# One decoder layer on one core: the calls of all five engines' programs in another sequence, with other fillers on TensorE

## The chip, the cores and the metric

The kernel runs on one NeuronCore of one Trainium2 chip. The metric is the device time of the whole program in microseconds (us); it counts from the first to the last activity on the core, with some 1.3 us around the span that the profile shows.

## The reference

The input x is 16 batches of 256 tokens by 512 channels, ctx a second tensor of the same shape. Cut to what matters:

```python
x = x + attention(layernorm(x))        # 16 heads of 32, one shared key and value head
x = x + wkv(w, u, layernorm(x), ctx)   # recurrence over the 256 tokens of a batch
x = x + ffn(layernorm(x))              # ternary weights, 2048 hidden units

# attention: windows of 128 queries, step 64, blended linearly where they overlap
K, V = quant_dequant_8bit(K), quant_dequant_8bit(V)   # min and max over ALL batches
p = sigmoid(scores); wout = (p / (p.sum(-1) + 1e-8)) @ V
# wkv: y = (A*p + E*vt) / (A*q + E), per channel, state carried from token to token
# ffn: activations rounded to 8 bit with a scale per token, weights to -1, 0, 1 with
#      one scale per matrix (a mean of absolute values), silu(gate) * up, RMS norm, down
```

Two facts of this set the order of the work at the start: keys and values are quantised with a minimum and maximum over all batches, so all of x must be loaded and projected before the first scores; and a weight can be rounded only when the sum over its whole matrix is known.

## The kernel before

The 16 batches are pipelined. Round b does the attention of batch b, the wkv of batch w = b−1, the first half (tokens 0 to 127, t = 0) of the hidden part of the FFN of f = b−2, and the second half (t = 1) of the hidden part and the down projection of g = b−3. Rounds 0 to 3 fill the pipeline and are written out call by call, rounds 4 to 15 are the body of a loop (`for i in range(4, B)`), and a tail empties it.

Each engine has a program of its own, a list of calls of small step functions written out by hand: `sync_program` (SP, which issues most DMAs), `tensor_program` (PE), `scalar_program` (ACT), `vector_program` (DVE) and `pool_program` (POOL). An engine does its steps strictly in the order of its list; steps of different engines meet only at semaphores. So a step that waits holds all that stands behind it in its own list. DMAs on SP's queue are issued in the order of SP's list, and each waits for its own condition first.

The steps that matter here, with the lines by which the profile names them:

- PE: `queries(b, t)` L558 projects the queries (with the residual's path folded in); `scores(b, h)` L577 for a group of four heads; `dens` L585 and `nums` L588 sum the probabilities and multiply them with the values; `attention_out` L608; `wkv_keys` L618 and `wkv_back` L627 transpose to and from the layout of the recurrence; `gate_up(f, t, n)` L646 is a chunk of 512 hidden units, eight products of gate and eight of up; `down(f, t, k)` L666 is half of the sum over the hidden units.
- PE's fillers: `spin(f, k, n)` L658 issues n products of a constant matrix into a bank that is free at that time. Nobody reads them. Each shows as two records in the trace.
- ACT: `keep_raw` L893 to 906 writes projected keys and values of two batches, `sum_weights` L914 adds up a chunk of 128x2048 weights, `set_keys` L928 dequantises keys; `probs` L945 is the sigmoid; `log_tables` L949 loads the function table for `logs` L956 and `inverses` L961 (a logarithm and an exponential that together make the reciprocal); `wkv_logs`, `wkv_inverses` L966, L971 do the same for the recurrence; `scale_tokens` L978, `scale_hidden` L984, `exps` L991, `silu` L1000, `squares` L1005.
- DVE: `round_weights` L1292 to 1301 makes ternary weights, three passes a chunk; `rope` L1378, `rotate` L1384, `blend_windows` L1392, `residual` L1402, `scan` L1425, `join` L1433, `refine` L1439, `quotient` L1446, the `wkv_...` steps up to L1492, `hidden(f, t, n)` L1503 (silu times up, out of PSUM), `peak` L1512, `hidden_scale` L1525, `hidden_round` L1532, `output` L1537.
- POOL: `weigh_windows` L1846, `weigh_hidden` L1863, `hidden_rstd` L1869, `outputs` L1883.
- SP: `load_x` L270 and `load_columns` L276 (x and its transpose, 1.05 MB a call), `load_weights` L293 (1.05 MB), `load_queries` L305, `load_residual` L300 (0.52 MB), `load_keys` L317, `turn_queries` L330, `turn_tokens` L337, `turn_hidden` L344 (transposes by DMA), `store` L351.

The fillers' code:

```python
def spin(f, k, n):
    if k >= 4:
        te.wait_ge(silu_set.sem, silu_set.at(f, (k - 4) // 2))
    ...
    for _ in range(n):
        te.matmul(bank[4 + k % 4][:, 0:S], ident[:, :], blend[:, 0:S], start=True, stop=True)
```

## Time and profile before

| | |
|---|---|
| time, median of 3 runs | 1019.5 us (1018.1 to 1020.02) |
| the profiled execution | 1018.47 us, its span 1017.2 us |
| PE, DVE busy | 899.2 us (88%), 876.8 us (86%) |
| ACT, POOL busy | 657.0 us (65%), 427.2 us (42%) |
| fillers (L658) | 318 records, 75.3 us of PE |

The profile is of one execution. The page divides the span into 40 slices and gives busy shares, bandwidth and the clock that TensorE was granted; the trace behind it has each instruction, and for idle time in front of an instruction the one whose semaphore ended it. Busy shares are averages over three stages: the start, the steady rounds, the tail.

### The profile page before, as it was taken

How to read it: one execution, taken by the hardware profiler on the slowest of the kernel's cores; microseconds unless marked ns; L12 is line 12 of the kernel's file. 1: busy time of each engine (PE TensorE's matmuls, PEld its weight loads, DVE VectorE, ACT ScalarE, POOL GpSimd, SP SyncE). 2: the span in 40 equal slices, each digit the busy share in tenths (PEclk: the TensorE clock that was granted, in tenths of full speed). 3: DMA queues.
4: the chain of work that ended last, by engine and by line, in shares of the span. 5: the costliest groups of instructions: out<-in, count | busy, mean ns of one | idle time of the engine just before them, and what ended most of it. 6: DMA issues, size and time to landing. Idle time of an engine off the chain costs nothing.

```text
span 1017.2 us, 22672 instructions
## 1 busy us (share of the span) xinstructions
PE 899.2 (88%) x8616; PEld 559.4 (55%) x8706; DVE 876.8 (86%) x1614; ACT 657.0 (65%) x1163; POOL 427.2 (42%) x494
## 2 busy tenths in 40 slices
PE   4997969977789998989898989898989898988898
PEld 2446657754455555555555555565555555555354
DVE  2866694799899999999999999989898989889884
ACT  0238554366666868686868685859585959595653
POOL 1200213116344454545454545454535363636452
PEclk9999989978899999999999999999999999999999
DMA  9986560020331323232323232415151515131132
GB/s 330 362 348 194 199 208 26 17 65 16 73 102 43 111 63 111 56 112 61 107 66 105 68 108 63 112 57 119 53 123 53 122 53 123 53 85 53 42 73 83
DMA packets 119389, 107.21 MB, mean 105 GB/s; under 512 B 91792, under 2 KB 94720, under 8 KB 118128
## 3 DMA queue, kind: packets, MB, share of 16 engines
q1 hardware_dynamic: 116320, 100.64, 33.1%
q0 software_dynamic: 624, 2.59, 0.7%
q10 hardware_dynamic: 2336, 2.52, 0.7%
q8 instruction: 69, 1.13, 0.5%
q14 instruction: 40, 0.33, 0.1%
HBM read 65.62 MB, written 10.75 MB: 75 GB/s over the span
## 4 chain that ended last, share of the span: by engine, by line
PE 37%; ACT 17%; POOL 14%; DVE 12%; issue 12%; DMA 2%; SPq 1%; DVEq 0%; POOLq 0%; ACTq 0%
PE bank L558 10%; PE bank L666 6%; POOL work L1863 5%; PE bank L646 5%; POOL sums L1846 4%; ACT arena L945 4%; PE bank L577 4%; PE bank L658 3%; PE bank L608 3%; ACT junk L1000 2%; ACT L949 2%; PE bank L585 2%; DVE wide L1358 2%; DVE amax L1468 2%; POOL sums L1883 2%
## 5 line engine op out<-in xcount | busy, mean ns | idle before, releaser
L1863 POOL TENSOR_TENSOR work<-junk,lnw 128x512 f32<-128x512 f32 x128 | 171.1, 1356 | 201.6 <-DVE junk L1503 176.8
L646 PE MATMUL bank<-w_up_gate,qT 128*128 128x512 bf16 x974 | 231.7, 383 | 19.1 <-DVE junk L1503 10.9
L646 PEld LDWEIGHTS bank<-w_up_gate,qT 128*128 128x128 bf16 x1024 | 95.6, 98 | 128.3 <-DVE junk L1503 21.7
L984 ACT ACTIVATE work<-work,fs 128x2048 f32<-128x2048 f32 x32 | 64.0, 2001 | 118.3 <-DVE fs L1525 118.3
L945 ACT ACTIVATE arena<-bank 128x384 f32<-128x384 f32 x256 | 104.8, 497 | 33.5 <-PE bank L577 33.3
L666 PE MATMUL bank<-w_down,work 128*128 128x512 bf16 x472 | 114.4, 387 | 11.3 <-ACT junk L1000 5.1
L558 PE MATMUL bank<-wide,wq_sb 128*128 128x256 f32 x512 | 114.5, 381 | 2.5 <-DVE rows L1402 2.5
L608 PE MATMUL bank<-wo_sb,wide 128*128 128x512 f32 x256 | 112.7, 592 | 1.2 <-DVE wide L1395 1.2
L558 PEld LDWEIGHTS bank<-wide,wq_sb 128*128 128x128 f32 x512 | 96.1, 190 | 26.0 <-issue 13.4
L577 PE MATMUL bank<-wide,k_win 32*128 32x128 f32 x1536 | 64.1, 298 | 47.1 <-ACT arena L945 23.4
L1005 ACT ACTIVATE junk<-junk 128x512 f32<-128x512 f32 x128 | 80.3, 627 | 39.2 <-DVE junk L1503 38.9
L1846 POOL TENSOR_TENSOR sums<-sums,blend 128x448 f32<-128x448 f32 x64 | 84.2, 1333 | 42.7 <-ACT sums L961 42.6
L1000 ACT ACTIVATE junk<-bank,deq 128x512 f32<-128x512 f32 x128 | 84.5, 681 | 23.7 <-PE bank L646 11.5
L1503 DVE TENSOR_TENSOR junk<-bank,junk 128x512 f32<-128x512 f32 x128 | 86.3, 683 | 13.1 <-POOL work L1863 8.1
L577 PEld LDWEIGHTS bank<-wide,k_win 32*128 32x128 f32 x1536 | 51.9, 195 | 74.7 <-ACT arena L945 42.9
L666 PEld LDWEIGHTS bank<-w_down,work 128*128 128x128 bf16 x512 | 46.5, 99 | 62.1 <-issue 6.3
L608 PEld LDWEIGHTS bank<-wo_sb,wide 128*128 128x128 f32 x256 | 48.5, 190 | 56.5 <-issue 53.1
L1425 DVE TENSOR_TENSOR_SCAN sums<-wkv_s,sums 128x256 f32<-128x256 f32 x128 | 77.8, 674 | 0.2 <-ACT sums L991 0.2
L658 PE MATMUL bank<-blend,ident 128*128 128x256 f32 x318 | 75.3, 390 | 0.0
L1512 DVE TENSOR_REDUCE fs<-work 128x1 f32<-128x2048 f32 x32 | 72.9, 2277 | 1.7 <-POOL work L1863 1.7
L1883 POOL TENSOR_TENSOR sums<-sums 128x512 f32<-128x512 f32 x32 | 41.0, 1283 | 73.5 <-ACT sums L971 66.0
L658 PEld LDWEIGHTS bank<-blend,ident 128*128 128x128 f32 x318 | 61.2, 195 | 11.4 <-issue 1.9
(156 smaller groups left out, 1614.0 us busy)
## 6 DMA issues: line engine op xcount, KB each, us to landing
sums<-in_xT SPq DMA_DIRECT2D x8, 1024.0 KB, 9.4
wide<-in_xT SPq DMA_DIRECT2D x16, 512.0 KB, 4.7
wide<-wide SPq DMA_DIRECT2D x64, 128.0 KB, 2.1
out<-rows SPq DMA_DIRECT2D x32, 256.0 KB, 2.3
rows<-in_x SPq DMA_DIRECT2D x15, 512.0 KB, 3.5
ctx_T<-in_ctxT SPq DMA_DIRECT2D x15, 512.0 KB, 3.7
...
```

The costliest lines, as they stand in the source:

```text
L558: last = te.matmul(in_bank(k, 2)[:, n % 2, :], wq_sb[:, c, n * P:(n + 1) * P], xT[:, c, :], start=c == 0, stop=c == NC - 1)
L577: last = te.matmul(bank[j][:, n * P:(n + 1) * P], k_win[head, window], q_cos[head, c, window], start=True, stop=True, skip_group_check=True)
L608: last = te.matmul(bank[t][:, :], heads_T[:, c, t * P:(t + 1) * P], wo_sb[:, c, :], start=c == 0, stop=c == NC - 1)
L646: last = te.matmul(bank[4 + k % 4][:, :], qT[:, c, t * P:(t + 1) * P], w_up_gate[:, m, c, cols], start=c == 0, stop=c == NC - 1)
L658: te.matmul(bank[4 + k % 4][:, 0:S], ident[:, :], blend[:, 0:S], start=True, stop=True)
L666: last = te.matmul(bank[6 + t][:, :], hid_T[:, t, c, :], w_down[:, c, :], start=c == 0, stop=c == NI - 1)
L945: se.activation(prob[:, :, QUAD * c + j, :], bank[j][:, 0:NW * P].rearrange("p (k q) -> p k q", k=NW), ACT.Sigmoid, scale=float(1.0 / np.s ...
L1000: se.activation(gated[:, n % 2, :], bank[4 + 2 * (n % 2)][:, :], ACT.Silu, scale=deq[:, 0, t:t + 1]).then_inc(silu_set.sem, 1)
L1005: se.activation(gated[:, n % 2, :], hid[:, n % 2, :], ACT.Square, accum_out=fs[:, t, n:n + 1]).then_inc(sq_set.sem, 1)
L1503: ve.tensor_tensor(hid[:, n % 2, :], bank[4 + k % 4][:, :], gated[:, n % 2, :], op=ALU.mult).then_inc(hid_set.sem, 1)
L1846: ge.tensor_tensor(soft[:, c, :], soft[:, c, :], blend[:, :], op=ALU.mult).then_inc(weighted.sem, 1)
L1863: ge.tensor_tensor(hid_w[:, t, cols], hid[:, n % 2, :], lnw[:, cols], op=ALU.mult).then_inc(z_set.sem, 1)
```

## The change

Every engine's list is written in another sequence. The steps are the same ones, with two exceptions: the number and places of the filler products change, and so does which of ACT's function tables is loaded when (the explicit load `log_tables(2, 0)` goes from round 2 to the head of the list). Calls at the loop's seams move from one side of its edge to the other. The core of the diff (left out are the rest of the start of DVE's and POOL's lists, and those of their tails):

```diff
@@ -377,110 +377,109 @@
             for t in range(NT):
                 sy.wait_ge(out_stored[t].sem, out_stored[t].at(B - 1))
 
-        load_x(1)
         load_columns(0)
-        load_columns(2)
         load_small()
         load_x(0)
+        load_x(1)
+        load_columns(2)
         load_columns(1)
         load_x(2)
         load_x(3)
         load_columns(3)
         load_x(4)
-        load_columns(5)
         load_columns(4)
         store_trig(0)
         load_x(5)
+        load_x(6)
+        load_columns(5)
+        load_x(7)
         load_columns(6)
-        load_x(6)
+        store_trig(2)
+        load_columns(7)
         load_wq()
-        load_keys(0)
-        load_columns(7)
-        load_x(7)
-        load_weights(GATE, 2)
+        load_queries(0)
+        next_residual(1)
         load_weights(GATE, 0)
         load_weights(GATE, 1)
-        load_queries(0)
+        load_weights(GATE, 3)
         store_trig(3)
-        load_weights(GATE, 3)
+        load_weights(GATE, 2)
+        load_keys(0)
         turn_queries(0, 0)
...
         queries(0, 0)
         queries(0, 1)
-        spin(0, 0, 5)
+        spin(0, 0, 6)
         scores(0, 0)
-        spin(0, 0, 6)
+        spin(0, 0, 7)
         scores(0, 1)
+        spin(0, 0, 1)
         scores(0, 2)
         spin(0, 0, 2)
         scores(0, 3)
+        spin(0, 0, 8)
         dens(0, 0)
         dens(0, 1)
+        nums(0, 0)
         dens(0, 2)
-        nums(0, 0)
+        spin(0, 0, 3)
         dens(0, 3)
-        spin(0, 0, 7)
+        spin(0, 0, 4)
         nums(0, 1)
         nums(0, 2)
-        spin(0, 0, 10)
+        spin(0, 0, 5)
         nums(0, 3)
         attention_out(0, 0)
         attention_out(0, 1)
-        spin(0, 0, 8)
         queries(1, 0)
         queries(1, 1)
+        spin(0, 0, 9)
         wkv_keys(0)
+        spin(0, 0, 15)
         scores(1, 0)
-        spin(0, 0, 4)
+        spin(0, 0, 10)
         scores(1, 1)
+        spin(0, 0, 11)
         scores(1, 2)
-        spin(0, 0, 3)
+        spin(0, 0, 12)
         scores(1, 3)
         dens(1, 0)
+        spin(0, 0, 13)
         dens(1, 1)
+        spin(0, 0, 14)
         dens(1, 2)
-        spin(0, 0, 9)
+        dens(1, 3)
         nums(1, 0)
-        spin(0, 0, 11)
         nums(1, 1)
-        dens(1, 3)
         nums(1, 2)
-        spin(0, 0, 12)
         nums(1, 3)
+        spin(0, 0, 16)
         wkv_back(0, 0)
         wkv_back(0, 1)
         attention_out(1, 0)
-        spin(0, 0, 13)
+        spin(0, 0, 17)
         attention_out(1, 1)
         queries(2, 0)
-        spin(0, 2, 7)
+        spin(0, 0, 18)
+        gate_up(0, 0, 0)
+        queries(2, 1)
         wkv_keys(1)
...
         for i in range(4, B):
-            b, w, f, g, h = i, i - 1, i - 2, i - 3, i - 4
+            b, w, f, g = i, i - 1, i - 2, i - 3
+            dens(w, 0)
+            dens(w, 1)
+            gate_up(g, 1, 0)
             dens(w, 2)
-            down(h, 1, 1)
             nums(w, 0)
             nums(w, 1)
             dens(w, 3)
             nums(w, 2)
+            nums(w, 3)
             gate_up(g, 1, 1)
-            nums(w, 3)
             gate_up(g, 1, 2)
             wkv_back(f, 0)
             wkv_back(f, 1)
@@ -811,6 +815,7 @@
             gate_up(f, 0, 1)
             wkv_keys(w)
             gate_up(f, 0, 2)
+            spin(f, 6, 2)
             gate_up(f, 0, 3)
             scores(b, 0)
             down(g, 0, 0)
@@ -819,17 +824,17 @@
             scores(b, 2)
             down(g, 1, 0)
             scores(b, 3)
-            gate_up(f, 1, 0)
-            dens(b, 0)
-            dens(b, 1)
+            down(g, 1, 1)
...
@@ -849,11 +853,12 @@
         down(13, 0, 1)
         down(13, 1, 1)
         gate_up(14, 1, 1)
+        spin(14, 12, 5)
         gate_up(14, 1, 2)
         wkv_back(15, 0)
         wkv_back(15, 1)
         gate_up(14, 1, 3)
-        spin(14, 16, 19)
+        spin(14, 16, 18)
         gate_up(15, 0, 0)
         gate_up(15, 0, 1)
         gate_up(15, 0, 2)
@@ -866,10 +871,9 @@
         gate_up(15, 1, 1)
         gate_up(15, 1, 2)
         gate_up(15, 1, 3)
-        spin(15, 16, 2)
         down(15, 0, 0)
         down(15, 0, 1)
-        spin(15, 16, 14)
+        spin(15, 16, 19)
         down(15, 1, 0)
...
+        log_tables(2, 0)
         load_tables()
         keep_raw(0)
         keep_raw(1)
         keep_raw(2)
         keep_raw(3)
         keep_raw(4)
-        wkv_tables()
         load_first_residual()
-        load_first_values()
+        sum_weights(GATE, 0)
         keep_raw(5)
-        sum_weights(GATE, 0)
         keep_raw(6)
         keep_raw(7)
         sum_weights(GATE, 1)
         sum_weights(GATE, 2)
+        sum_weights(GATE, 3)
+        wkv_tables()
         set_keys(0)
-        sum_weights(GATE, 3)
         probs(0, 0)
         probs(0, 1)
-        log_tables(0, 0)
         probs(0, 2)
         probs(0, 3)
+        log_tables(0, 0)
         logs(0, 0)
+        sum_weights(UP, 0)
         inverses(0, 0)
         logs(0, 1)
-        sum_weights(UP, 0)
         logs(0, 2)
+        load_first_values()
         logs(0, 3)
...
         silu(0, 0, 2)
-        squares(0, 0, 1)
         silu(0, 0, 3)
         probs(2, 0)
+        log_tables(1, 0)
         probs(2, 1)
+        squares(0, 0, 2)
         probs(2, 2)
-        squares(0, 0, 2)
...
         for i in range(4, B):
             b, w, f, g = i, i - 1, i - 2, i - 3
-            silu(g, 1, 1)
-            silu(g, 1, 2)
-            squares(g, 1, 1)
-            silu(g, 1, 3)
+            scale_tokens(f)
             scale_hidden(g, 0)
-            squares(g, 1, 2)
             set_keys(b)
-            scale_tokens(f)
-            squares(g, 1, 3)
             scale_hidden(g, 1)
             silu(f, 0, 0)
             silu(f, 0, 1)
@@ -1172,13 +1176,13 @@
             logs(b, 3)
             inverses(b, 3)
             silu(f, 1, 0)
+            silu(f, 1, 1)
             squares(f, 1, 0)
-        silu(13, 1, 1)
-        silu(13, 1, 2)
-        squares(13, 1, 1)
-        silu(13, 1, 3)
-        squares(13, 1, 2)
-        squares(13, 1, 3)
+            silu(f, 1, 2)
+            squares(f, 1, 1)
+            silu(f, 1, 3)
+            squares(f, 1, 2)
+            squares(f, 1, 3)
...
@@ -1614,11 +1618,11 @@
         wkv_quantise(0)
         residual(1)
         wkv_round(0)
+        round_weights(DOWN, 0)
         att_norm(1)
         wkv_steps(0)
-        round_weights(DOWN, 0)
+        hidden(0, 0, 0)
         round_weights(DOWN, 1)
-        hidden(0, 0, 0)
         rope(2, 0)
...
         for i in range(4, B):
             b, w, f, g, h = i, i - 1, i - 2, i - 3, i - 4
+            join(f)
             keys_grid(b)
             peak(g, 0)
             refine(f, 0)
+            output(h, 0)
             refine(f, 1)
             output(h, 1)
             quotient(f, 0)
@@ -1703,58 +1707,58 @@
             hidden_round(g, 0)
             hidden(f, 0, 0)
             rope(b, 0)
+            hidden(f, 0, 1)
             hidden_round(g, 1)
-            hidden(f, 0, 1)
             rope(b, 1)
             rotate(b, 0)
+            scan(w, 0)
             values(w)
-            scan(w, 0)
+            rotate(b, 1)
             scan(w, 1)
-            rotate(b, 1)
             hidden(f, 0, 2)
             hidden(f, 0, 3)
-            output(g, 0)
-            join(w)
+        join(14)
+        peak(13, 0)
```

The first place is in TensorE's list, at attention_out of batch 0 (L608, L607 after the change) and the scores, sums and products of batch 1 behind it. Before:

```order
L608 MATMUL bank<-wo_sb,wide 128x512 x8
L658 MATMUL bank<-blend,ident 128x256 x8
L558 MATMUL bank<-wide,wq_sb 128x256 x16
L618 MATMUL bank<-ident,wide 128x128 x8
L577 MATMUL bank<-wide,k_win 128x128 x12
L658 MATMUL bank<-blend,ident 128x256 x4
L577 MATMUL bank<-wide,k_win 128x128 x24
L658 MATMUL bank<-blend,ident 128x256 x3
L577 MATMUL bank<-wide,k_win 128x128 x12
L585 MATMUL bank<-arena,one_win 32x128 x12
```

After:

```order
L607 MATMUL bank<-wo_sb,wide 128x512 x8
L557 MATMUL bank<-wide,wq_sb 128x256 x16
L657 MATMUL bank<-blend,ident 128x256 x9
L617 MATMUL bank<-ident,wide 128x128 x8
L657 MATMUL bank<-blend,ident 128x256 x15
L576 MATMUL bank<-wide,k_win 128x128 x12
L657 MATMUL bank<-blend,ident 128x256 x10
L576 MATMUL bank<-wide,k_win 128x128 x12
L657 MATMUL bank<-blend,ident 128x256 x11
L576 MATMUL bank<-wide,k_win 128x128 x12
L657 MATMUL bank<-blend,ident 128x256 x12
L576 MATMUL bank<-wide,k_win 128x128 x12
```

Ahead of and among the scores and the sums stand 9, 15, 10, 11, 12, 13 and more filler products where 8, 4, 3, 9 and more stood.

The second place is in TensorE's list too, in a steady round: gate_up(f, 0, 2) and (f, 0, 3), the scores of batch b with down between them, and the sums of batch b behind them. Before:

```order
L646 MATMUL bank<-w_up_gate,qT 128x512 x16
L577 MATMUL bank<-wide,k_win 128x128 x12
L666 MATMUL bank<-w_down,work 128x512 x8
L577 MATMUL bank<-wide,k_win 128x128 x12
L666 MATMUL bank<-w_down,work 128x512 x8
L577 MATMUL bank<-wide,k_win 128x128 x12
L666 MATMUL bank<-w_down,work 128x512 x8
L577 MATMUL bank<-wide,k_win 128x128 x12
L646 MATMUL bank<-w_up_gate,qT 128x512 x8
L585 MATMUL bank<-arena,one_win 32x128 x12
L588 MATMUL bank<-arena,one_win 32x64 x4
```

After:

```order
L645 MATMUL bank<-w_up_gate,qT 128x512 x8
L657 MATMUL bank<-blend,ident 128x256 x2
L645 MATMUL bank<-w_up_gate,qT 128x512 x8
L576 MATMUL bank<-wide,k_win 128x128 x12
L665 MATMUL bank<-w_down,work 128x512 x8
L576 MATMUL bank<-wide,k_win 128x128 x12
L665 MATMUL bank<-w_down,work 128x512 x8
L576 MATMUL bank<-wide,k_win 128x128 x12
L665 MATMUL bank<-w_down,work 128x512 x8
L576 MATMUL bank<-wide,k_win 128x128 x12
L665 MATMUL bank<-w_down,work 128x512 x8
L584 MATMUL bank<-arena,one_win 32x128 x12
```

Two fillers stand between gate_up(f, 0, 2) and (f, 0, 3), the last half of down comes before the first sums, and gate_up(f, 1, 0) between the second and third instead of ahead of the first.

The third place is the end of TensorE's list: the last chunks of gate_up of batch 15 and its down. Before:

```order
L646 MATMUL bank<-w_up_gate,qT 128x512 x40
L666 MATMUL bank<-w_down,work 128x512 x32
L646 MATMUL bank<-w_up_gate,qT 128x512 x24
L658 MATMUL bank<-blend,ident 128x256 x2
L666 MATMUL bank<-w_down,work 128x512 x16
L658 MATMUL bank<-blend,ident 128x256 x14
L666 MATMUL bank<-w_down,work 128x512 x16
```

After:

```order
L645 MATMUL bank<-w_up_gate,qT 128x512 x40
L665 MATMUL bank<-w_down,work 128x512 x32
L645 MATMUL bank<-w_up_gate,qT 128x512 x24
L665 MATMUL bank<-w_down,work 128x512 x16
L657 MATMUL bank<-blend,ident 128x256 x19
L665 MATMUL bank<-w_down,work 128x512 x16
```

The two fillers ahead of down are gone, and 19 stand between its halves instead of 14.

## Rows read from the trace of the kernel before

**Rows 1.** The page: its head, and the bandwidth of the 40 slices.

```profile
span 1017.2 us, 22672 instructions
...
GB/s 330 362 348 194 199 208 26 17 65 16 73 102 43 111 63 111 56 112 61 107 66 105 68 108 63 112 57 119 53 123 53 122 53 123 53 85 53 42 73 83
```

**Rows 2.** TensorE timeline: start us, us, line, out<-in, count [idle before <-releaser].

```profile
14.68 1.56 PE L534 MATMUL bank<-arena 128*128 128x96 f32 x6 [14.68 <-DMA arena<-in_low_rank]
...
74.25 7.13 PE L558 MATMUL bank<-wide,wq_sb 128*128 128x256 f32 x32
...
115.78 7.13 PE L608 MATMUL bank<-wo_sb,wide 128*128 128x512 f32 x16 [1.20 <-DVE wide L1395]
...
141.13 1.24 PE L577 MATMUL bank<-wide,k_win 32*128 32x128 f32 x16 [6.98 <-DVE wide L1384]
...
185.40 3.60 PE L608 MATMUL bank<-wo_sb,wide 128*128 128x512 f32 x8
```

**Rows 3.** ScalarE timeline at 67 us, columns as in the group before.

```profile
67.40 1.91 ACT L914 ACTIVATE junk<-work 128x2048 f32<-128x2048 f32 x1 [0.41 <-ACT q_tok L904]
```

**Rows 4.** ScalarE groups, 84.9 to 115.8 us: count | busy, mean ns | idle before.

```profile
L945 ACT ACT_TABLE_LOAD x2 | 2.6, 1283 | 1.8 <-PE bank L577 1.8
L956 ACT ACT_TABLE_LOAD x2 | 2.6, 1283 | 0.0
L961 ACT ACT_TABLE_LOAD x2 | 2.6, 1283 | 0.0
L956 ACT ACTIVATE sums<-bank,sum_eps 128x448 f32<-128x448 f32 x4 | 2.4, 630 | 0.0
L949 ACT ACT_TABLE_LOAD x1 | 1.3, 1283 | 0.0
```

**Rows 5.** Windows: stretch, PE, PEld, DVE, ACT, POOL busy, PEclk, DMA share, GB/s.

```profile
115.80:189.00 73.20, 61.87 (x553) 47.12 (x554) 51.62 (x84) 32.01 (x53) 15.12 (x16) 0.95 0.28 92
189.00:313.80 124.80, 104.15 (x1015) 66.69 (x1026) 112.28 (x182) 77.02 (x135) 49.93 (x53) 0.90 0.19 56
```

**Rows 6.** Windows of line L658 alone: PE, PEld busy, PEclk, DMA share, GB/s.

```profile
115.78:189.03 73.25, 28.44 (x120) 23.03 (x120) 0.95 0.28 92
```

**Rows 7.** VectorE timeline, 199 to 204 us.

```profile
199.77 1.28 DVE L1292 TENSOR_SCALAR work<-work,w_scale 128x2048 f32<-128x2048 f32 x1
...
202.35 1.23 DVE L1301 TENSOR_SCALAR w_down<-work 128x2048 bf16<-128x2048 f32 x1
203.49 0.68 DVE L1503 TENSOR_TENSOR junk<-bank,junk 128x512 f32<-128x512 f32 x1
```

**Rows 8.** TensorE timeline: two waits of rounds 2 and 3.

```profile
238.65 1.25 PE L585 MATMUL bank<-arena,v_win 128*32 128x128 f32 x17 [4.14 <-ACT sums L956]
...
260.16 1.03 PE L646 MATMUL bank<-w_up_gate,qT 128*128 128x512 bf16 x4 [1.26 <-DMA qT<-q_tok]
```

**Rows 9.** TensorE timeline, a steady round at 534 us.

```profile
533.94 1.04 PE L646 MATMUL bank<-w_up_gate,qT 128*128 128x512 bf16 x4 [0.67 <-DVE junk L1503]
...
535.93 0.95 PE L577 MATMUL bank<-wide,k_win 32*128 32x128 f32 x24 [0.95 <-DVE wide L1384]
```

**Rows 10.** The chain that ended last: start us, us, engine, line.

```profile
313.84 7.13 PE bank L558 x32
...
519.22 7.14 PE bank L558 x32
...
570.55 7.14 PE bank L558 x32
...
589.28 4.11 DMA wide<-wide
...
879.78 7.14 PE bank L558 x32
```

**Rows 11.** TensorE timeline, the tail.

```profile
1004.18 6.21 PE L658 MATMUL bank<-blend,ident 128*128 128x256 f32 x28
1010.68 1.46 PE L666 MATMUL bank<-w_down,work 128*128 128x512 bf16 x6 [0.30 <-DMA work<-work]
```

More of the change, by code:

```diff
@@ L1084, in scalar_program @@
         wkv_logs(1, 0)
+        logs(2, 1)
         wkv_logs(1, 1)
         wkv_inverses(1, 0)
+        inverses(2, 1)
         wkv_inverses(1, 1)
[L1088 removed]
         logs(2, 2)
         silu(0, 1, 0)
[L1091 to L1093 removed]
+        inverses(2, 2)
         logs(2, 3)
[L1095 removed]
         inverses(2, 3)
         silu(0, 1, 1)
+        squares(0, 1, 0)
         silu(0, 1, 2)
         squares(0, 1, 1)
+        silu(0, 1, 3)
         squares(0, 1, 2)
[L1101 to L1102 removed]
         scale_hidden(0, 0)
         scale_tokens(1)
+        squares(0, 1, 3)
         set_keys(3)
@@ L1574, in vector_program @@
         rotate(0, 0)
-        rotate(0, 1)
         weight_mean(GATE)
         round_weights(GATE, 0)
+        rotate(0, 1)
         round_weights(GATE, 1)
         round_weights(GATE, 2)
+        round_weights(GATE, 3)
         blend_windows(0, 0)
-        round_weights(GATE, 3)
+        keys_grid(1)
         blend_windows(0, 1)
@@ L1591, in vector_program @@
         rope(1, 0)
+        rope(1, 1)
         round_weights(UP, 2)
-        rope(1, 1)
         rotate(1, 0)
+        round_weights(UP, 3)
         values(0)
-        round_weights(UP, 3)
+        rotate(1, 1)
         scan(0, 0)
-        rotate(1, 1)
         scan(0, 1)
```

294 lines of the change are left out of this document (142 added, 152 removed).

## The prediction

> **What bounds the kernel now.** I read the page first, then the chain that ended last, then timelines of each engine stretch by stretch. The page's head gives a span of 1017.2 us; the profiled execution took 1018.5 in all, and the median of the runs shown is 1.0 above that, so my sum is made on 1018.5 and gets 1.0 added at its end. The bandwidth row shows the first stage: three slices at 330 to 362 GB/s [rows 1], with nearly all of x under way. No score can start before x is in. The chain then shows the steady rounds by their anchor, the 32 products of queries: 313.84 to 879.78 us are 11 rounds, 51.45 us each, an undisturbed one (519.22 to 570.55) 51.33 [rows 10]. Between lies the filling of the pipeline, 81.4 us (end of queries(0, ·), 74.25 + 7.13) to 313.8 [rows 2, 10], and the change touches this most.
>
> In that filling two stretches differ. From 115.8 to 189.0 TensorE is busy 61.87 of 73.20 us, of which 28.44 us are fillers that nobody reads; from 189.0 to 313.8 VectorE is the full one, 112.28 of 124.80 us [rows 5, 6]. In a steady round no engine is always busy: a loop of hand-overs goes from queries over gate_up, silu and the sigmoids to the reciprocals of the recurrence, POOL's products, VectorE's rounding and back to queries.
>
> **The change, stage by stage.**
>
> *1. Start to the end of queries(0, ·): −2.7.* The first products wait for low_rank [rows 2], which goes out behind x1, col0 and col2 (3.1 MB) and in future behind col0 alone. Two loads of 1.05 MB and what POOL loads beside them, together 2.5 MB, at 347 GB/s (mean of the first three slices, [rows 1]) make 7.2 us by which projections can start earlier. But all of x must come, and its bytes are the same. GATE weight 0 lands behind x, its transpose, wq, 0.5 MB for queries and 0.5 for the residual, about 21.4 MB with the small loads: at 347 GB/s and 2 us to begin, 63.7 us. Its sum now stands ahead of keep_raw(5) on ScalarE, where today it starts at 67.40, right behind keep_raw(5)'s copies [rows 3]; so keep_raw(5) can't be done much before 66 us. load_keys(0) stands behind all four weights. Bounds: −7.2 (nothing of it lost) and 0; I take −2.7, nearer to nothing, since keep_raw(5) by this sum comes when it comes now.
>
> *2. To the start of attention_out(0, 0): −3.7.* ScalarE loads its table seven times between 84.9 and 115.8 us, each 1.28 us [rows 4], as log_tables(0, 0) stands between the second and third sigmoid group and the later sigmoids throw its table out. Behind all four groups it is loaded twice: 5 fewer, −6.4. ScalarE is what the sums wait for here. Fillers in the stretch go from 30 to 36. A filler costs 28 records / 2 = 14 in 6.21 us, 0.444 us [rows 11]; six are +2.7. Bounds −6.4 and +2.7.
>
> ScalarE's next activation follows a load with no idle time [rows 4]. The Trainium skill (ScalarE: Activation LUTs, What ACT_TABLE_LOAD costs) puts a drain of some 1.38 us to each load, 2.66 in all; by that the five would give −13.3 and the sum would be 6.9 us lower. No such gap shows in the rows, and the sum goes by them.
>
> *3. attention_out(0, 0) to the end of attention_out(1, 1): +12.8.* This is the main term. Now it is 115.78 to 185.40 + 3.60 = 189.0, 73.2 us [rows 2]. Fillers in it: 8+4+3+9+11+12+13 = 60 (120 records, 28.44 us); in future 9+15+10+11+12+13+14+16+17 = 117. TensorE's list is strict, and these products depend on nothing that comes late, so they are a floor: 117 × 0.444 = 51.9. The other work of the stretch is 61.87 − 28.44 = 33.4 [rows 5, 6]. Together 85.3, and 0.7 for short waits: 86.0. The 11.3 us that TensorE idles now, 6.98 of them ahead of the scores at 141.13 [rows 2], are thereby filled up and overrun. Bounds: 85.3 − 73.2 = +12.1, if no wait is left, and +57 × 0.444 = +25.3, if all waits stay. They can't: 24 fillers (10.7 us) now stand ahead of scores(1, 0), where rope and rotate cost a wait of 6.98.
>
> *4. To hidden(0, 0, 0): +3.7.* From 189.0 to hidden's start at 203.49 are 14.5 us [rows 2, 7]. In future 18 fillers (8.0) instead of 7 (3.1) stand ahead of gate_up(0, 0, 0), while wkv_keys (1.1) goes behind it: gate_up starts some 3.8 us later, and as hidden is held today by round_weights up to 203.58 and not by TensorE [rows 7], it comes at the same distance. But VectorE's list has hidden(0, 0, 0) ahead of round_weights(DOWN, 1): it waits for TensorE first, and the chunk, three passes from 199.77 to 203.58, 3.8 us [rows 7], is still to do, with VectorE the full engine of what follows. Bounds 0 (the late TensorE gives VectorE slack elsewhere) and +3.8; I take +3.7.
>
> *5. To queries(4, ·) at 313.84: −4.0.* TensorE's wait of 4.14 us for logs(2, 3) [rows 8] goes, since squares(0, 1, 0) and a table load no longer stand ahead of it on ScalarE; the 1.26 us for a transpose of tokens [rows 8] is covered by queries(3, 1), which moves ahead of gate_up(1, 0, 0); hidden_rstd(1, 0) and outputs move up on POOL, the recurrence's steps on VectorE. If all of that counted, −8.5; VectorE is busy 90% of the stretch [rows 5], so −8.5 can't be had whole. I take the middle of 0 and −8.5. Later fillers (6+3+1 = 10, in future 2+4+5 = 11) change nothing.
>
> *6. Eleven steady rounds: −1.0.* In the loop's list of TensorE two fillers (0.89) come ahead of gate_up(f, 0, 3). There TensorE waits 0.67 us for VectorE's hidden in the middle of the chunk and 0.95 for rotate before the scores [rows 9]: 1.62 us of cover for 0.89. If that cover were gone they would cost 0.9 a round, 9.8 in all. down(g, 1, 1), gate_up(f, 1, 0) and the sums change places; the hand-overs by which they wait (the last transposes of g, silu) came a microsecond or more earlier in the trace. On SP, turn_queries(b, 1) now stands behind two transposes instead of four; in the disturbed rounds the chain goes through such a transpose, 4.11 us at 589.28 [rows 10]. What the 11 rounds have above 11 undisturbed ones is 565.94 − 564.63 = 1.3; I take 1.0 of it. output(h, 0) goes from the end of VectorE's body to its head, off the loop of hand-overs in both places.
>
> *7. Tail: +2.3.* Between down(15, 0, 1) and down(15, 1, 0) TensorE spends 6.21 us on fillers and waits 0.30 for the transposed hidden units [rows 11]. 19 fillers last 8.4 us, and the transpose has long been there: +1.9. 5 fillers ahead of gate_up(14, 1, 2) and 18 instead of 19 further on against four and two that go: +0.4.
>
> **Sum:** −2.7 − 3.7 + 12.8 + 3.7 − 4.0 − 1.0 + 2.3 = +7.4. 1018.5 + 7.4 + 1.0 = 1026.9, forecast **1027 us**, slower. Its own range is 1022.5 (terms 1, 2 and 5 nearer their good ends) to 1031.
>
> **The rivals.**
>
> *A, faster: the round gets shorter.* If the round is set by VectorE's list and not by the loop of hand-overs, the covered waits count: 0.67 us at the chunk [rows 9], and an output (0.7 us, as long as hidden's pass in [rows 7]) ahead of join, 1.4 a round, −15.4 over eleven: 1011.5. It turns the sign from −7.5 / 11 = −0.68 a round on. Against it: in the chain of an undisturbed round VectorE has only rounding and residual, and waits for POOL.
>
> *B: the start's gain is kept whole*, −7.2 instead of −2.7: 1022.5. For it: ScalarE idles for microseconds between the projections now. Against it: bytes, as in step 1.
>
> *C: the rounds get longer.* turn_hidden(g, 0, 1) and (g, 1, 1) now go out later on SP, each behind a wait of another kind. If down(g, ·, 1) waits 0.5 to 1.0 us for them each round, with scores and sums behind it on TensorE, the time is 1032.5 to 1038.
>
> *Clock.* TensorE was granted 0.95 of its full clock from 115.8 to 189.0 and 0.90 up to 313.8 [rows 5]: in part of them it ran at 1.2 instead of 2.4 GHz. With fillers where it idled, it could be granted all of it. A stretch wholly at full speed takes at most 5% off the 61.87 us of its work, 3 us: 1024. The Trainium skill (TensorE: Matmul & The Clock Gate, Part 1) says that a busy TensorE keeps the full clock, and it speaks for this rival; the rows of the fillers alone show the same 0.95 [rows 6].
>
> *D: a table load costs the 2.66 us of the Trainium skill's page on ScalarE*: 1020. Against it stands the idle time of 0.0 behind the loads [rows 4].
>
> **How the numbers follow.** Forecast 0.55, A 0.10, B 0.13, C 0.12, clock 0.05, D 0.02, others 0.03. A difference of 0.2%, 2 us, is about what a measurement of this kernel can tell from none. Faster by that (below 1017.5) are A and some of the others: 0.13. Within it fall D and combinations in which terms 1, 2 and 5 all come at their good ends: 0.10. Slower 0.77. The range leaves out most of A below and the upper half of C above: 1018 to 1034.
>
> **What would show each step.** 1: first product near 7.5 us, queries(0, ·) ending near 78.5. 2: two table loads between there and attention_out(0, 0), and this 34.3 to 30.6 us behind. 3: from attention_out(0, 0) to the end of (1, 1) 86 us with 234 filler records, and under 2 us idle; if it is below 85, the fillers are cheaper than I hold. 4: VectorE waiting for TensorE ahead of hidden(0, 0, 0), and a chunk of DOWN behind it. 5: no wait of microseconds for logs(2, 3), and queries(4, ·) near 320. 6: rounds of 51.3 to 51.4; 50 would be rival A, 52 or more with waits ahead of down L665 rival C. 7: 38 records of fillers in front of the last 16 products, and no wait behind them. The prediction fails if the rounds move by more than 0.5 us, since eleven of them outweigh every other term, or if the loss of step 3 is given back by VectorE, which could use the time for work that binds it later.

## The result, and the profile after

The changed kernel takes 1030.64 us in the median of 4 runs (1028.07 to 1030.83), the kernel before 1019.21 beside it. The ratio is 1.0095, with a 95% interval of 1.007 to 1.012 (the two medians alone give 1.0112): slower, as forecast (1027, range 1018 to 1034). The profiled execution took 1030.51 us, its span is 1029.2, 12.0 above that of before. The head of its page:

```profile
span 1029.2 us, 23167 instructions
```

The same anchors as in [rows 10] and [rows 2], now from the changed kernel: first the chain that ended last, then TensorE's timeline (L557 is queries, L607 attention_out). A line with x3 shows the first three products of a group:

```profile
317.87 7.13 PE bank L557 x32
...
684.82 7.14 PE bank L557 x32
...
737.10 7.14 PE bank L557 x32
...
894.00 7.15 PE bank L557 x32
```

```profile
7.46 0.93 PE L533 MATMUL bank<-arena 128*128 128x96 f32 x3 [7.46 <-DMA arena<-in_low_rank]
...
66.43 7.13 PE L557 MATMUL bank<-wide,wq_sb 128*128 128x256 f32 x32
...
105.81 7.13 PE L607 MATMUL bank<-wo_sb,wide 128*128 128x512 f32 x16 [1.21 <-DVE wide L1399]
115.45 0.89 PE L557 MATMUL bank<-wide,wq_sb 128*128 128x256 f32 x3 [2.51 <-DVE rows L1406]
...
190.71 3.60 PE L607 MATMUL bank<-wo_sb,wide 128*128 128x512 f32 x8
```

The differences of these starts, stage by stage:

| stage | before | after | moved | forecast |
|---|---|---|---|---|
| 1 start to end of queries(0, ·) | 81.4 | 73.6 | −7.8 | −2.7 |
| 2 to attention_out(0, 0) | 34.4 | 32.2 | −2.2 | −3.7 |
| 3 to the end of attention_out(1, 1) | 73.2 | 88.5 | +15.3 | +12.8 |
| 4, 5 to queries(4, ·) | 124.8 | 123.6 | −1.3 | −0.3 |
| 6 eleven rounds | 565.9 | 576.1 | +10.2 | −1.0 |
| 7 tail | 137.4 | 135.2 | −2.2 | +2.3 |

The sum was off by 4.6 us, but its terms by up to 11: the time lies in the range because a gain at the start and in the tail, and a loss in the rounds, all three far beyond what I had forecast, nearly cancel. That part of the hit is luck. The experiments are about stages 3, 6 and 1. Medians below are compared with 1030.6 of the changed kernel; ratios are to runs of the kernel before beside them, whose median was 1018.8 to 1020.4, so differences between medians of two experiments are good to some 2 us.

**Where the rounds lose.** An undisturbed round takes 52.28 us (684.82 to 737.10), before 51.33. In both kernels TensorE gets to the scores 16.5 to 16.7 us into the round, ScalarE loads its table at 28.9, and POOL starts weigh_windows at 33.6: none of the three moved. What comes later is the end of VectorE's list. Between the layernorm after attention and that after wkv VectorE does the same 66 instructions. First the windows and groups of VectorE in the kernel before, then after (columns as in [rows 5] and [rows 4]; join is L1433 before and L1437 after, refine L1439 and L1443):

```profile
525.30:564.38 39.08, 35.14 (x466) 21.20 (x472) 38.20 (x66) 32.29 (x58) 20.91 (x20) 1.00 0.35 107
```

```profile
L1433 DVE SCALAR_TENSOR_TENSOR sums<-sums,wkv_s 128x512 f32<-128x512 f32 x4 | 3.7, 993 | 0.0
...
L1439 DVE TENSOR_TENSOR sums<-sums 128x512 f32<-128x512 f32 x2 | 2.0, 1019 | 0.0
```

```profile
690.91:730.97 40.06, 36.77 (x476) 22.06 (x476) 39.72 (x66) 32.97 (x60) 21.75 (x19) 1.00 0.35 104
```

```profile
L1437 DVE SCALAR_TENSOR_TENSOR sums<-sums,wkv_s 128x512 f32<-128x512 f32 x4 | 4.4, 1160 | 0.0
L1443 DVE TENSOR_TENSOR sums<-sums 128x512 f32<-128x512 f32 x2 | 2.9, 1470 | 0.0
```

VectorE is busy 39.72 us instead of 38.20 with the same work: join +0.7, refine +0.9, the last step of blend_windows +0.4, and small gains against them. Its idle time falls from 0.88 to 0.34, and the stretch grows by 0.98. The timelines of POOL and VectorE in the changed kernel show beside what they run:

```profile
708.26 2.96 POOL L1867 TENSOR_TENSOR work<-junk,lnw 128x512 f32<-128x512 f32 x2 [7.74 <-DVE junk L1507]
716.45 1.18 POOL L1887 TENSOR_TENSOR sums<-sums 128x512 f32<-128x512 f32 x1 [5.23 <-ACT sums L975]
718.42 4.26 POOL L1850 TENSOR_TENSOR sums<-sums,blend 128x448 f32<-128x448 f32 x3 [0.78 <-ACT sums L965]
...
728.73 3.74 POOL L1867 TENSOR_TENSOR work<-junk,lnw 128x512 f32<-128x512 f32 x3 [0.89 <-DVE junk L1507]
```

```profile
708.68 4.41 DVE L1437 SCALAR_TENSOR_TENSOR sums<-sums,wkv_s 128x512 f32<-128x512 f32 x4
...
716.59 1.59 DVE L1443 TENSOR_TENSOR sums<-sums 128x512 f32<-128x512 f32 x1
718.10 0.74 DVE L1541 SCALAR_TENSOR_TENSOR rows<-bank,fs,rows 128x512 f32<-128x512 f32 x1
718.76 1.35 DVE L1443 TENSOR_TENSOR sums<-sums 128x512 f32<-128x512 f32 x1
```

Join starts 0.42 us behind the start of two products of weigh_hidden (L1867) and lies beside them for 2.5 us; the first refine lies beside POOL's step `outputs` (L1887), the second, pushed back by VectorE's `output` (L1541) of 0.74, beside weigh_windows (L1850). In round 1, with POOL idle, the same passes are short, a refine 0.69 us for 1.59 and 1.35 here:

```profile
145.17 2.71 DVE L1437 SCALAR_TENSOR_TENSOR sums<-sums,wkv_s 128x512 f32<-128x512 f32 x4
...
159.48 0.69 DVE L1443 TENSOR_TENSOR sums<-sums 128x512 f32<-128x512 f32 x1 [0.62 <-ACT sums L975]
```

POOL in its turn, which ran without a break from weigh_windows up to rstd_wkv before, now waits 0.89 us for VectorE at 728.73. The chain that ended last says the same. Ahead of rstd_wkv, the last long piece of work in it is weigh_hidden on POOL before, and on VectorE after:

```profile
563.60 2.50 POOL work L1863 x2
```

```profile
678.76 1.19 DVE stats_wkv L1462 x2
```

### The profile page after: what moved, and what is told of

Read it like the earlier page. It is cut to its first block, busy times and chain, and to the rows that moved or that the text cites. A ratio compares the mean times of both kernels' runs of the same rounds, so it can differ in the third digit from the quotient of the medians.

```text
span 1029.2 us, 23167 instructions
## 1 busy us (share of the span) xinstructions
PE 945.8 (92%) x8910; PEld 594.2 (58%) x8910; DVE 887.2 (86%) x1614; ACT 656.1 (64%) x1160; POOL 437.3 (42%) x494
## 3 DMA queue, kind: packets, MB, share of 16 engines
q8 instruction: 70, 1.15, 0.5%
## 4 chain that ended last, share of the span: by engine, by line
PE 24%; ACT 15%; DVE 15%; issue 9%; POOL 8%; DMA 2%; SPq 1%; DVEq 0%; ACTq 0%; POOLq 0%
PE bank L557 8%; PE bank L665 7%; POOL sums L1850 5%; PE bank L645 5%; ACT arena L949 4%; PE bank L576 3%; DVE junk L1507 3%; ACT L953 2%; ACT junk L1004 2%; POOL sums L1887 2%; DVE amax L1472 2%; DVE stats_wkv L1462 2%; ACT sums L970 1%; DMA wide<-wide 1%; DVE wide L1362 1%
## 5 line engine op out<-in xcount | busy, mean ns | idle before, releaser
L1867 POOL TENSOR_TENSOR work<-junk,lnw 128x512 f32<-128x512 f32 x128 | 182.8, 1445 | 193.3 <-DVE junk L1507 168.2
L645 PE MATMUL bank<-w_up_gate,qT 128*128 128x512 bf16 x1024 | 238.8, 379 | 11.0 <-DVE junk L1507 7.7
L665 PE MATMUL bank<-w_down,work 128*128 128x512 bf16 x512 | 121.6, 384 | 6.0 <-ACT junk L1004 5.1
L657 PE MATMUL bank<-blend,ident 128*128 128x256 f32 x522 | 121.2, 384 | 0.0
L557 PE MATMUL bank<-wide,wq_sb 128*128 128x256 f32 x512 | 114.3, 381 | 4.1 <-DVE rows L1406 3.3
L607 PE MATMUL bank<-wo_sb,wide 128*128 128x512 f32 x256 | 112.7, 593 | 1.2 <-DVE wide L1399 1.2
L557 PEld LDWEIGHTS bank<-wide,wq_sb 128*128 128x128 f32 x512 | 96.1, 190 | 28.0 <-issue 15.5
L657 PEld LDWEIGHTS bank<-blend,ident 128*128 128x128 f32 x522 | 98.4, 191 | 16.8 <-issue 1.2
L1850 POOL TENSOR_TENSOR sums<-sums,blend 128x448 f32<-128x448 f32 x64 | 85.2, 1345 | 46.0 <-ACT sums L965 46.0
L1507 DVE TENSOR_TENSOR junk<-bank,junk 128x512 f32<-128x512 f32 x128 | 86.0, 680 | 10.6 <-ACT junk L1004 5.2
L607 PEld LDWEIGHTS bank<-wo_sb,wide 128*128 128x128 f32 x256 | 48.5, 190 | 56.5 <-issue 53.1
L982 ACT ACTIVATE wide<-wide,amax 128x512 f32<-128x512 f32 x32 | 21.3, 714 | 80.7 <-DVE amax L1476 80.7
```

Of the source, the lines that this page charges most:

```text
L557: last = te.matmul(in_bank(k, 2)[:, n % 2, :], wq_sb[:, c, n * P:(n + 1) * P], xT[:, c, :], start=c == 0, stop=c == NC - 1)
L607: last = te.matmul(bank[t][:, :], heads_T[:, c, t * P:(t + 1) * P], wo_sb[:, c, :], start=c == 0, stop=c == NC - 1)
L645: last = te.matmul(bank[4 + k % 4][:, :], qT[:, c, t * P:(t + 1) * P], w_up_gate[:, m, c, cols], start=c == 0, stop=c == NC - 1)
L665: last = te.matmul(bank[6 + t][:, :], hid_T[:, t, c, :], w_down[:, c, :], start=c == 0, stop=c == NI - 1)
L1507: ve.tensor_tensor(hid[:, n % 2, :], bank[4 + k % 4][:, :], gated[:, n % 2, :], op=ALU.mult).then_inc(hid_set.sem, 1)
L1850: ge.tensor_tensor(soft[:, c, :], soft[:, c, :], blend[:, :], op=ALU.mult).then_inc(weighted.sem, 1)
```

## The experiments

**e1 and e2: the place of output(h, 0) in VectorE's loop.**

```diff
+            output(h, 0)       # e1
             join(f)
+            output(h, 0)       # e2, instead of the line of e1
             keys_grid(b)
             peak(g, 0)
             refine(f, 0)
-            output(h, 0)
             refine(f, 1)
```

> The changed kernel, with output(h, 0) moved from between the two refines back to ahead of join(f) in VectorE's loop, and nothing else. Theory 1 (where join and refine stand beside POOL's products sets their length): join falls from 4.4 to 3.75 us a round and the two refines from 2.9 to 2.0, rounds go from 52.29 to 51.3-51.4, and the time from 1030.6 to 1020-1021. Theory 2 (the two loop fillers or the new order of scan, values and rotate make the round longer): rounds stay at 52.2-52.3 and the time at 1030.

Measured: 1020.44 us, ratio 0.9998 (0.9979 to 1.0017); rounds of 51.35; join 3.75, refines 1.84 together in the round at 524.49 us, up to 2.19 in others. Theory 1 holds. All that the rounds lost comes back with one call of 0.7 us moved by some places.

> The changed kernel, with output(h, 0) right behind join(f). Theory 1 splits here: join starts as early as in the changed kernel, so it stays at 4.4 us, but the refines lie together again as before, though 0.7 us later and so nearer to POOL's products: 2.0 to 2.9 us for both. Rounds of 51.5 to 52.1, time 1022 to 1028. If only the output's own 0.7 us between the refines counted, it would be no different from its other places: 1030.6 or 1020.

Measured: 1019.97 us, ratio 0.9989 (0.9967 to 1.0011), rounds of 51.35. VectorE's timeline, POOL's, and the last long piece of the chain in e2:

```profile
699.71 4.38 DVE L1437 SCALAR_TENSOR_TENSOR sums<-sums,wkv_s 128x512 f32<-128x512 f32 x4
...
708.25 1.55 DVE L1443 TENSOR_TENSOR sums<-sums 128x512 f32<-128x512 f32 x2
...
710.38 0.97 DVE L1450 SCALAR_TENSOR_TENSOR sums<-sums 128x512 f32<-128x512 f32 x1
```

```profile
699.27 2.95 POOL L1867 TENSOR_TENSOR work<-junk,lnw 128x512 f32<-128x512 f32 x2 [7.73 <-DVE junk L1507]
707.46 1.19 POOL L1887 TENSOR_TENSOR sums<-sums 128x512 f32<-128x512 f32 x1 [5.24 <-ACT sums L975]
709.43 4.15 POOL L1850 TENSOR_TENSOR sums<-sums,blend 128x448 f32<-128x448 f32 x3 [0.78 <-ACT sums L965]
```

```profile
720.23 2.50 POOL work L1867 x2
```

Join takes 4.38 us beside weigh_hidden as in the changed kernel, so what lengthens join and what lengthens the refines are two things, and the forecast for join was right. The refines start only 0.8 us behind POOL's outputs and use the pause of 0.78 us ahead of weigh_windows: 1.55 for both, less than before or in e1. My range for the time (1022 to 1028) was too high: rounds of e1 and e2 are equal to 0.01 us, and the chain goes over POOL again, so VectorE is not what sets them in either. Here are two lines of VectorE and one of POOL in e1:

```profile
556.60 1.84 DVE L1443 TENSOR_TENSOR sums<-sums 128x512 f32<-128x512 f32 x2
...
559.02 0.97 DVE L1450 SCALAR_TENSOR_TENSOR sums<-sums 128x512 f32<-128x512 f32 x1
```

```profile
556.11 1.18 POOL L1887 TENSOR_TENSOR sums<-sums 128x512 f32<-128x512 f32 x1 [4.88 <-ACT sums L975]
```

Join is 0.6 us longer in e2, and yet quotient (L1450) starts 34.5 us into the round in both and in the kernel before, each time 1.73 or 1.74 us behind the end of POOL's product of L1887 (L1883 before). What join takes longer, the refines wait less. So join's growth costs nothing. In the changed kernel quotient starts 3.07 us behind the end of that product, 1.34 more: about half is the output of 0.7 us itself, which elsewhere lies in time for which the refines wait anyway, and half the second refine, 1.35 us where it would take 0.6 to 0.7 in POOL's pause.

**e13: output(h, 0) behind both refines.**

```diff
             refine(f, 0)
-            output(h, 0)
             refine(f, 1)
+            output(h, 0)
```

> The changed kernel with output(h, 0) behind refine(f, 1). The same work again, at a third place. Theory 1 (contention with POOL): join stays at 4.4, the first refine beside POOL's product at 1.6 us, the second lies in POOL's pause between its output and weigh_windows and takes 0.7 to 1.0: rounds 51.6 to 51.9, time 1023 to 1026. If it were the delay of quotient by an output in front of it, it would be as slow as the changed kernel, 1030.6, since two outputs stand in front of quotient in both.

Measured: 1029.53 us, ratio 1.0081 (1.0055 to 1.0107), rounds of 52.05. The expectation failed in size. VectorE, then POOL:

```profile
718.08 2.19 DVE L1443 TENSOR_TENSOR sums<-sums 128x512 f32<-128x512 f32 x2
720.20 1.40 DVE L1541 SCALAR_TENSOR_TENSOR rows<-bank,fs,rows 128x512 f32<-128x512 f32 x2
721.52 1.42 DVE L1450 SCALAR_TENSOR_TENSOR sums<-sums 128x512 f32<-128x512 f32 x1
```

```profile
717.94 1.18 POOL L1887 TENSOR_TENSOR sums<-sums 128x512 f32<-128x512 f32 x1 [5.23 <-ACT sums L975]
719.91 4.04 POOL L1850 TENSOR_TENSOR sums<-sums,blend 128x448 f32<-128x448 f32 x3 [0.78 <-ACT sums L965]
```

The first refine starts 0.14 us behind the start of POOL's product, as in the changed kernel, instead of 0.8 as in e2. Both together take 2.19, and it is quotient (L1450) that now takes longest beside weigh_windows, 1.42 us for 0.97 in e2. The lengths of the refines come out as a wait for POOL's product to end and then the passes: in e13 POOL's ends at 719.12, 1.04 behind the refine's start, and 1.15 us are left for two passes; in e2 it ends 0.40 behind, and 1.15 us are left again; in the changed kernel 1.04 behind, and 0.55 are left for one. The Trainium skill (SBUF — State Buffer, SBUF: two separate sides) says just this, that a GpSimd instruction that reads SBUF and a VectorE instruction with two SBUF inputs take a common port exclusively, each for its whole length; these rows agree, by the 1.15 and 0.55 us that are left. So the slowing goes on to whichever pass on two SBUF operands stands there; the outputs, with one operand in PSUM, stay at 0.74. Of the two ways of reading in the expectation, the time speaks for the second (what stands in front of quotient), the durations for the first; as I read it they are one thing, since two outputs in front of quotient push it further into POOL's long run.

The traces also show the price of a delay. The first pass of quotient ends 35.50 us into the round before, in e1 and in e2, 36.62 in e13 and 36.85 in the changed kernel. The rounds take 51.35 (51.33 before), 52.05 and 52.28. So a delay of 1.12 us costs 0.70 and one of 1.35 costs 0.93: the first 0.4 us are free. That fits the wait of 0.39 us for weigh_hidden that VectorE has before and in e2, and no longer has in the changed kernel.

**e3: no fillers in the loop.** The call `spin(f, 6, 2)` is left out.

> The changed kernel without spin(f, 6, 2) in TensorE's loop. Theory 1 (the fillers fill a wait that is there anyway, as step 6 of the prediction has it): rounds stay at 52.29, time 1030 to 1031. Theory 2 (they are what makes the round longer): 0.89 us a round come back, 1021.

Measured: 1030.33 us, ratio 1.0096 (1.0066 to 1.0126), rounds of 52.27. Theory 1 holds: the two products that nobody reads cost nothing, and the scores wait for rotate behind them (0.72 us at 701.33 in the changed kernel, 0.95 before in [rows 9]).

**e4, e10, e5: the stretch from attention_out(0, 0) to (1, 1).** e4 has the counts of before in the new places, e10 TensorE's old list in the stretch, e5 no filler:

```diff
         attention_out(0, 1)
+        spin(0, 0, 8)          # e10
         queries(1, 0)
         queries(1, 1)
-        spin(0, 0, 9)          # e4: 8, e10 and e5: none
         wkv_keys(0)
-        spin(0, 0, 15)         # e4: 4, e10 and e5: none
         scores(1, 0)
-        spin(0, 0, 10)         # e4: 3, e10: 4, e5: none
         scores(1, 1)
-        spin(0, 0, 11)         # e4, e10 and e5: none
         scores(1, 2)
...
```

> The changed kernel with the filler counts of the kernel before in the stretch from attention_out(0, 0) to attention_out(1, 1): 60 products, not 117. If the stretch is set by TensorE's list alone, 57 x 0.444 = 25.3 us of fillers go and waits come back; with 73 to 76 us for 88.5 the time is 1015.5 to 1018. If VectorE, full behind this stretch, had used the time for work that it must do anyway, part comes back as waits later: 1020 to 1025.

> The changed kernel, with TensorE's list from attention_out(0, 0) to attention_out(1, 1) as in the kernel before, word for word: 60 fillers and in their old places, and with the old order of the sums and products of batch 1. The other engines' lists stay changed. With 60 fillers in the new places the stretch took 83.3 us of 88.5 against 73.2 before. Theory 1 (the rest is in the places: fillers that stand between queries(1, .) and wkv_keys(0) hold rope, and fillers after waits run at the low clock): 73 to 76 us, time 1016 to 1019. Theory 2 (the rest comes from the changed lists of ScalarE and POOL, behind whose inverses the quotient waits): 80 to 83 us, time 1023 to 1025.

> The changed kernel with no fillers from attention_out(0, 0) to attention_out(1, 1). 117 of them take 52 us in the changed kernel, and 60 in the same places left the stretch at 83.3 us for 88.5, with a granted clock of 0.87. Theory 1 (the waits of the other engines are the floor): 36 us of other work on TensorE, at the low clock 45 to 50, and waits of 25 or more: 76 to 80 us, time 1018 to 1021. Theory 2 (without fillers TensorE stays at the low clock for longer, and products on the way of the other engines are late): as long as with 60, 1024.

Measured: e4 1024.66 us, ratio 1.0035 (1.0012 to 1.0057); e10 1018.26, 0.9992 (0.9975 to 1.001); e5 1015.18, 0.9945 (0.9919 to 0.9971). The stretch in windows, of the changed kernel, then e4, e10 and e5:

```profile
105.81:194.31 88.50, 84.92 (x667) 67.40 (x668) 50.29 (x80) 28.73 (x49) 14.38 (x15) 1.00 0.23 74
```

```profile
105.19:188.51 83.32, 67.40 (x553) 50.72 (x554) 51.35 (x80) 29.21 (x49) 14.85 (x15) 0.88 0.25 79
```

```profile
105.46:181.90 76.44, 63.78 (x553) 48.70 (x554) 51.31 (x80) 29.25 (x49) 14.90 (x15) 0.91 0.27 86
```

```profile
105.96:179.27 73.31, 41.54 (x433) 29.39 (x434) 51.35 (x80) 28.80 (x49) 14.85 (x15) 0.74 0.29 89
```

The second number of each line is TensorE's busy time, the last but two its mean clock. With 117 fillers TensorE is busy 84.92 of 88.50 us at the full clock. Without any it is busy 41.54 us of 73.31 with a mean clock of 0.74, so for about half of the time at 1.2 GHz, and the stretch takes what it took before with 60 [rows 2]. I read this so that the other engines need those 73 us and TensorE's 32 us of waits hide the low clock; no run shows it by itself. 60 fillers take 76.4 us in their old places and 83.3 in the new ones, at 0.91 and 0.88. Theory 1 of e4 missed: 5.2 us came back in the stretch instead of 13. The time lies in the range of its second theory (1020 to 1025), but not for that reason: what the rest waits for is not work that VectorE had done meanwhile. It is the order of TensorE's list, above all fillers ahead of wkv_keys, scores and sums that others need; e10 says so (76.4 us, and 1018.3 in theory 1's range). e10 also has the old order of dens(1, 3) and the products of batch 1, which was not tried apart from the fillers' places. Of +15.3 us, 5.2 are the count, 6.9 the places with that order, and 3.2 what is left, which I put down to the lists of the other engines. Each share is good to some 2 us: in traces of kernels with the changed kernel's lists here the stretch takes 88.5 to 88.6 us (the changed kernel, e2, e8) or 90.1 to 90.9 (e1, e3, e6, e7, e12, e13). The medians say the same: −6.0, −12.4 and −15.5 (by the ratios −6, −10.5 and −15). e5's theory 1 was right in kind and 3 us too high.

**e6: 14 fillers in the tail,** `spin(15, 16, 14)` for `spin(15, 16, 19)`.

> The changed kernel with 14 fillers ahead of the last half of down, for 19. In the changed kernel's trace no wait stands behind the 19 (8.37 us); the transposed hidden units landed before. If they landed as long after the first half as in the kernel before (6.5 us), 5 x 0.444 = 2.2 us less fillers give 1.9 back: 1028.7. If they landed later, no difference.

Measured: 1030.27 us, ratio 1.0114 (1.009 to 1.0137). The end of TensorE's timeline, after and in e6:

```profile
1014.49 8.37 PE L657 MATMUL bank<-blend,ident 128*128 128x256 f32 x38
1022.69 3.62 PE L665 MATMUL bank<-w_down,work 128*128 128x512 bf16 x16
```

```profile
1013.62 6.21 PE L657 MATMUL bank<-blend,ident 128*128 128x256 f32 x28
1021.51 3.61 PE L665 MATMUL bank<-w_down,work 128*128 128x512 bf16 x16 [1.68 <-DMA work<-work]
```

With 14 a wait of 1.68 us shows up: the transposed hidden units land 7.9 us behind the first half, not 6.5 as in [rows 11]. The five fillers cost 0.3 us, not 1.9.

**e8, e7, e12: the start.** e8 puts x1 and col2 back ahead of the small weights. e7 puts the sum over GATE 0 behind keep_raw(7). e12 has all of SP's old start:

```diff
# e8, SP's list
+        load_x(1)
         load_columns(0)
+        load_columns(2)
         load_small()
         load_x(0)
-        load_x(1)
-        load_columns(2)
...
# e7, ScalarE's list
-        sum_weights(GATE, 0)
         keep_raw(5)
         keep_raw(6)
         keep_raw(7)
+        sum_weights(GATE, 0)
```

> The changed kernel with its first loads in the order of before: x1, col0 and col2 ahead of the small weights, the rest of SP's list unchanged. Theory 1 (the first product at 7.5 us instead of 14.7 is what gains the 7.8 us of the start): queries(0, .) ends at 80 to 81 us instead of 73.6, and the time is 1037. Theory 2 (the gain comes from the order of the later loads and of ScalarE's sums): it ends at 74 to 75, time 1030 to 1032.

> The changed kernel with the sum over GATE 0 behind keep_raw(5) to (7) on ScalarE. Step 1 of the prediction held that this sum, ahead of keep_raw(5), eats up most of the start's gain. If it does at all, ScalarE's wait of 4.5 us for it at 58.04 goes, keep_raw(5) comes at about 56 instead of 59.95, and queries(0, .) ends 1 to 3 us earlier: 1028 to 1029.5. If the last columns of x set the end, it is 73.6 as now, 1030.6.

> The changed kernel with the start of SP's list (all loads up to the last of GATE, and the residual behind the first transposes) as in the kernel before; ScalarE's list stays changed, with the sum over GATE 0 ahead of keep_raw(5). Restoring the first three loads alone moved the end of queries(0, .) from 73.6 to 76.0. Theory 1 (the whole gain of the start, 7.8 us, comes from SP's order: the DMA engines never idle between loads): it ends at 81 or later, the sum over GATE 0 now coming later too, and the time is 1038 to 1042. Theory 2 (the rest of the gain lies in ScalarE's list): 76 to 77, 1033.

Measured: e8 1033.44 us, ratio 1.0138 (1.0108 to 1.0168), queries(0, ·) ending at 75.95; e7 1031.09, 1.0106 (1.0077 to 1.0135); e12 1051.29, 1.0297 (1.0267 to 1.0327), ending at 92.4. Windows of the start, before and after; what SP waited for up to 66 us (in total, times, longest), before and after; and the bandwidth before in slices of 1.5 us from 0 to 60:

```profile
2.00:54.00 52.00, 37.80 (x124) 18.13 (x125) 28.84 (x80) 7.05 (x21) 10.21 (x18) 0.97 0.98 359
```

```profile
2.00:54.00 52.00, 45.07 (x153) 21.59 (x154) 34.32 (x99) 7.65 (x26) 12.16 (x20) 1.00 1.03 406
```

```profile
SPq L270 <- DVE stats_x L1249: 20.9, 3, 14.9
```

```profile
SPq L270 <- DVE stats_x L1253: 14.3, 3, 8.0
```

```profile
GB/s 0 121 412 403 376 273 227 421 404 428 404 418 407 421 197 371 328 426 137 216 418 273 418 330 384 400 415 423 416 403 412 394 392 294 316 371 408 429 437 421
```

From 2 to 54 us the core moves 406 GB/s for 359, and SP stands 14.3 us for free buffers of x instead of 20.9. The kernel before reached 400 to 428 GB/s too, but with gaps down to 137. With the gaps gone, x is in earlier, and so is everything behind it. ScalarE in the changed kernel, then TensorE in e7:

```profile
58.04 1.91 ACT L918 ACTIVATE junk<-work 128x2048 f32<-128x2048 f32 x1 [4.54 <-DMA work<-in_wgT]
```

```profile
66.19 8.81 PE L557 MATMUL bank<-wide,wq_sb 128*128 128x256 f32 x32
```

Without the sum in front, keep_raw(5) comes at 57.38 instead of 59.95, and yet queries(0, 0) starts at 66.19 for 66.43, with 66.0 to 66.2 in e1, e2, e3 and e6, which keep the sum in front: the sum ate nothing. (In e7 the 32 products took 8.81 us for 7.13, at a mean granted clock of 0.81, and the time did not fall.) The first loads are worth 2.4 us of the 7.8 by e8, between its two theories and nearer the second; its median is 2.8 above, from four runs that lie 5.5 us apart. e12 lies outside both of its theories and can't be used to share out the rest: the old loads seem not to fit the other engines' new lists, ScalarE waits 11.5 us for projections at 68.29, and queries end 11 us later than in the kernel before. How the other 5.4 us divide stays open.

**e11: what is left if the costly parts are taken out.** TensorE's stretch as in e10, output(h, 0) as in e2, 14 fillers in the tail.

> Three restorations in one: the stretch of TensorE's list as in e10, output(h, 0) behind join(f), 14 fillers in the tail for 19. If the three are independent, their gains add up: 10.6 for the output, 12 to 14 (theory 1) or 6 (theory 2) for the stretch, 1.9 for the tail: 1004 to 1007 by theory 1, 1012 by theory 2. Either would be faster than the kernel before.

Measured: 1007.58 us, ratio 0.9887 (0.9865 to 0.9909): 1.1% faster than the kernel before. The gains add up: 10.7 (e2), 12.4 (e10) and 0.4 (e6) off 1030.6 would be 1007.1. The time is 0.6 us above the range of theory 1, which had 1.9 for the tail.

## Why the prediction was right or wrong

The sign is right, and so is the largest term that was forecast, step 3, in kind. The number is in the range by luck: step 6 was off by +11.2 us, steps 1 and 7 by −5.1 and −4.5. By one of its own signs, "The prediction fails if the rounds move by more than 0.5 us", the account failed: they moved by 0.95.

*Step 1* was mis-sized: −7.8 for −2.7, the price of rival B. The failing term was "at 347 GB/s and 2 us to begin, 63.7 us" for GATE 0: the sum ran at 58.04, with the new order of loads at 406 GB/s. 347 was a mean of a page's row that contained SP's waits, and I took it for what the DMA engines can do. That the sum would hold keep_raw(5) was right for keep_raw(5) and without effect on the end (e7). The first product came at 7.46, as forecast.

*Step 2*: −2.2 for −3.7, in its bounds. Two table loads are left of seven, as forecast.

*Step 3*: +15.3 for +12.8. The floor was right, 84.9 us of work for 85.3, and the waits were 3.6 us for 0.7; 2.51 of them stand ahead of queries(1, ·), where the eight fillers had been. But a floor is no marginal cost: taking 57 fillers away gives 5.2 us, and the 60 that remain at their old places, with the old order around them, 12.1. I had reasoned with their number, and about half of the price is the order.

*Steps 4 and 5*: −1.3 for −0.3. hidden(0, 0, 0) starts 14.2 us behind the end of attention_out(1, 1), 14.5 before. VectorE does wait ahead of it, for ScalarE's silu of TensorE's late chunk, and the chunk of DOWN stands behind it, as step 4 said. Of step 5's two waits, the 4.14 us one is down to 1.42 and the one for the transpose is gone. How the −1.3 divides between the two steps was not tried.

```profile
208.56 0.69 DVE L1507 TENSOR_TENSOR junk<-bank,junk 128x512 f32<-128x512 f32 x1 [3.39 <-ACT junk L1004]
```

*Step 6* failed, and with it 11 us. The wrong sentence is: "output(h, 0) goes from the end of VectorE's body to its head, off the loop of hand-overs in both places." VectorE waits 0.88 us in 39 of a round and, by e13, only 0.4 us of delay ahead of quotient are free, so nothing there is off the loop by more than that; and I counted instructions at fixed lengths where they depend on what POOL does beside them. The part on the two fillers was right (e3). Rival C had the right price, 0.5 to 1.0 us a round, and the wrong mechanism: no wait for a transpose stands ahead of down. Rival A had the right engine and the wrong sign.

*Step 7*: −2.2 for +2.3. The fillers cost 0.3 by e6. Of the 4.5 us by which the term was off, that is 1.6. TensorE's wait for VectorE ahead of wkv_back(15, ·), 2.55 us before, is 0.38 after, which may be 2.2 more; neither this nor the remaining 0.7 was tried.

*Clock*: the granted clock in stage 3 rose from 0.95 to 1.00, as this rival had it, but the time did not fall: by e5 the fillers that hold the clock cost more than it gives, and the lowest mean clock goes with the shortest time. The clock alone is worth something: among the kernels with the same lists here, the 32 products of queries(1, ·) take 7.14 us at the full clock (the changed kernel, e2, e8) or 8.83 at a mean of 0.81 (e1, e6), and the stretch is 1.7 to 2.3 us longer in these two.

*Rival D*: stage 2 fell by 2.2 us. By the 2.66 us a load of the Trainium skill (ScalarE: Activation LUTs, What ACT_TABLE_LOAD costs), five loads fewer and six fillers more would have made it fall by an estimated 13.3 − 2.7 = 10.6 us, and the trace does not agree.
